# A six-layer transformer on one core: four of the repeated slots written out, and the hand order changed on every engine

## The reference

```python
xn = layernorm(x)
s = xn
for i in range(6):
    h = layernorm(s, ln1_w[i], ln1_b[i])
    q, k = softmax(h @ wq[i], over head dim), softmax(h @ wk[i], over tokens)
    s = (q @ (k.T @ (h @ wv[i]))) @ wo[i] + bo[i] + s      # 8 heads of 16
    h = layernorm(s, ln2_w[i], ln2_b[i]) @ w1[i]
    s = leaky_relu(h, 0.01) @ w2[i] + s                    # 128 -> 512 -> 128
logits = xn @ router_w.T + router_b
y = (xn @ expert_w[top1].T + expert_b[top1]) * max(softmax(logits))
out = x + s * silu(y)
```

## Time and profile before

| | |
|---|---|
| median of 3 runs | 595.34 us (593.69 to 601.31) |
| the profiled execution | 596.75 us, of which its span is 594.9 us |
| mean granted TensorE clock | 0.994 |
| PE busy | 578.7 us, 97% of the span |
| PE weight loads busy | 516.3 us, 87% |
| DVE busy | 540.1 us, 91% |
| ACT busy | 434.8 us, 73% |
| POOL busy | 311.1 us, 52% |

### The profile page before, as it was taken

One profiled execution on the slowest core, in us unless ns is written; L12 is line 12 of the kernel. 1 busy time (PEld: TensorE's weight loads), 2 busy tenths in 40 slices (PEclk: granted clock), 3 DMA queues, 4 the chain that ended last, 5 costly groups with the idle time before them and its releaser, 6 DMA issues.

```text
span 594.9 us, 12614 instructions
## 1 busy us (share of the span) xinstructions
PE 578.7 (97%) x4166; PEld 516.3 (87%) x4166; DVE 540.1 (91%) x1352; ACT 434.8 (73%) x763; POOL 311.1 (52%) x308
## 2 busy tenths in 40 slices
PE   7999999999999999999999999999999999999897
PEld 7899897887978889889889898898898898898796
DVE  6887999999988999999999999999999999988865
ACT  2658595876976868868768768768779678687652
POOL 5896134755852772442442532433523766867752
PEclk9989999999999999999999999999999999999999
DMA  8209233323224154445435435445342351441102
GB/s 282 75 10 328 72 110 121 124 94 130 95 84 152 71 152 146 112 133 169 124 123 163 109 141 150 116 163 158 103 165 80 108 167 57 129 156 62 45 36 106
DMA packets 74946, 73.20 MB, mean 123 GB/s; under 512 B 27265, under 2 KB 65153, under 8 KB 74882
## 3 DMA queue, kind: packets, MB, share of 16 engines
q1 hardware_dynamic: 72400, 68.18, 35.6%
q0 software_dynamic: 2048, 4.20, 2.3%
q10 hardware_dynamic: 434, 0.02, 0.0%
HBM read 39.87 MB, written 32.51 MB: 122 GB/s over the span
## 4 chain that ended last, share of the span: by engine, by line
PE 75%; DVE 11%; DMA 4%; issue 3%; POOL 3%; ACT 2%; SPq 1%; DVEq 0%; ACTq 0%; POOLq 0%
PE psY L513 23%; PE psH L406 6%; PE psS L558 6%; PE psH L407 6%; PE psH L408 6%; PE psT L592 6%; PE psT L401 6%; PE psT L526 5%; PE psM L538 5%; DVE st L1295 2%; PE psS L455 2%; DMA through<-blocks 1%; DVE X L1563 1%; DVE hid L1553 1%; DMA turned<-through 1%
## 5 line engine op out<-in xcount | busy, mean ns | idle before, releaser
L513 PE MATMUL psY<-w_all,hid 128*128 128x128 f32 x1536 | 188.7, 276 | 2.5 <-DVE hid L1553 1.8
L513 PEld LDWEIGHTS psY<-w_all,hid 128*128 128x128 f32 x1536 | 182.0, 193 | 6.6 <-issue 2.3
L1553 DVE TENSOR_TENSOR hid<-psH,hsl 128x512 f32<-128x512 f32 x192 | 127.2, 676 | 13.6 <-ACT hsl L936 13.1
L936 ACT ACTIVATE hsl<-psH 128x512 f32<-128x512 f32 x192 | 108.3, 591 | 42.0 <-PE psH L408 38.5
L2038 POOL TENSOR_TENSOR rstd<-veps,minus_half 128x8 f32<-128x8 f32 x44 | 72.7, 1653 | 61.2 <-DVE veps L1312 61.0
L2134 POOL TENSOR_TENSOR qsm<-qe,qrec 128x1024 f32<-128x1024 f32 x24 | 46.5, 1938 | 97.8 <-DVE qrec L1636 97.8
L2112 POOL TENSOR_TENSOR xn_lo<-xn,xn_hi 128x512 fp32r<-128x512 f32 x48 | 60.6, 1282 | 69.4 <-ACT xn_hi L1000 69.4
L406 PE MATMUL psH<-xn_hi,w_hi 128*128 128x512 f32 x192 | 86.4, 450 | 3.7 <-DVE hid L1553 3.4
L966 ACT ACTIVATE xh<-X,shift,rstd 128x128 f32<-128x128 f32 x188 | 77.0, 482 | 8.9 <-POOL shift L2041 8.7
L408 PE MATMUL psH<-xn_lo,w_hi 128*128 128x512 f32 x192 | 76.1, 396 | 0.0
L407 PE MATMUL psH<-xn_hi,w_lo 128*128 128x512 f32 x192 | 76.0, 396 | 0.0
(11 more groups left out here) (161 smaller groups left out, 1024.9 us busy)
## 6 DMA issues: line engine op xcount, KB each, us to landing
through<-turn SPq DMA_DIRECT2D x22, 512.0 KB, 2.7
turn<-through SPq DMA_DIRECT2D x88, 128.0 KB
through<-blocks SPq DMA_DIRECT2D x20, 512.0 KB, 3.2
turned<-through SPq DMA_DIRECT2D x80, 128.0 KB, 2.8
wb<-expert_rows SPq DMA_DIRECT2D x40, 128.0 KB, 2.0
sorted_x<-blocks SPq DMA_DIRECT2D x5, 512.0 KB, 4.4
xs_xsT<-sorted_x SPq DMA_DIRECT2D x40, 64.0 KB, 2.5
sorted_y<-ys SPq DMA_DIRECT2D x10, 256.0 KB, 2.4
```

What stands on the lines that cost most here:

```text
L513: last = nc.tensor.matmul(tile(psY, t), tile(hid[:, c, :], t), w2_all[:, n // NBATCH, c, :], start=(c == 0 and t == 0), stop=(c == NC - 1) ...
L936: nc.scalar.activation(hsl[:, i % 2, :], psH[:, i % 2, :], ACT.Copy, scale=SLOPE) \
L1553: nc.vector.tensor_tensor(hid[:, i % NC, :], psH[:, i % 2, :], hsl[:, i % 2, :], ALU.max) \
```

## The change

The helpers stay as they are; the calls are put in another order. On every engine the loop of slots ends at 20, and slots 20 to 23 are written out. POOL, DVE, PE, ACT and SP also have another order in the head, in the tail, and (POOL and DVE) inside the repeated slot. PE's set of calls is the same one, 618 of them. One `...` line stands for what is left out.

SP, the head:

```diff
-            sp.dma_start(w1_all[:, 0, :], w1[0]).then_inc(sig("ffn_first_loaded"), 16)
...
-            zero_rows()
             gather_expert_rows()
+            feature_major2(1)
+            zero_rows()
             sp.dma_start(w1_all[:, 1:L, :], w1[1:L].rearrange("l p f -> p l f")).then_inc(sig("ffn_loaded"), 16)
-            feature_major2(1)
-            feature_major2(2)
             for l in range(1, L):
                 sp.dma_start(w2_all[:, l, :, :], w2[l].rearrange("(p c) d -> p c d", c=NC)) \
                     .then_inc(sig("ffn_loaded"), 16)
+            feature_major2(2)
             feature_major1(4)
```

The head on PE and on DVE (pieces):

```diff
             first_items_by_feature(0)
+            normalised_tiles(0, 0)
             output_bias(0)
-            normalised_tiles(0, 0)
             keys(0)
...
-            attention(6)
             hidden(5, 0)
+            attention(6)
             hidden(5, 1)
             hidden(5, 2)
```

```diff
+            nc.vector.memset(eighths[:, :], 1.0 / H).then_inc(sig("ones_ready"), 1)
             input_statistics(0)
-            nc.vector.memset(ones256[:, :], 1.0)
             input_statistics(1)
             first_norm1_half(0)
...
+            add_y(1, 0)
+            leaky(1, 5)
             finish_mix(3)
-            leaky(1, 5)
             first_rows()
-            add_y(1, 0)
...
+            leaky(5, 0)
             add_attention(6)
-            leaky(5, 0)
-            leaky(5, 1)
             statistics2(6)
             key_maxima(7)
+            leaky(5, 1)
```

The repeated slot on POOL after (DVE's has `leaky(s - 3, 5)` ahead of `finish_mix(s - 1)` and `stage_w1` behind `add_attention`):

```diff
+                low_part(s - 3, 0)
                 if s % NBATCH == 3 and s < ITEMS:
                     split_w1(s // NBATCH)
-                low_part(s - 3, 0)
+                deviations2(s - 2)
                 low_part(s - 3, 1)
-                deviations2(s - 2)
```

PE in slot 20: `apply_expert(9)` stands behind `hidden(17, 3)` instead of ahead of `hidden(17, 0)`, and DVE's `expert_bias(9)` behind `variances1(20)`. PE in slots 20 to 22, as in slot 21 here:

```diff
             output(18, 2)
-            context(20)
             hidden(18, 4)
+            context(20)
             hidden(18, 5)
-            mixing(20)
             output(18, 3)
+            mixing(20)
             queries_by_feature(20)
```

The tail on ACT, DVE and POOL (pieces):

```diff
             slope(21, 4)
+            slope(21, 5)
             silu(0)
-            slope(21, 5)
+            silu(1)
+            queries_by_feature(23)
             slope(21, 6)
-            queries_by_feature(23)
```

```diff
             add_y(22, 1)
+            gated(2)
             leaky(23, 2)
             leaky(23, 3)
-            gated(2)
             leaky(23, 4)
             last_output(0)
```

```diff
             low_part(22, 1)
+            weigh(2)
+            deviations2(23)
             weigh(3)
-            deviations2(23)
-            add_input(0, 1)
             low_part(23, 0)
             low_part(23, 1)
             add_last_input()
+            add_input(0, 1)
             add_input(1, 2)
             add_input(2, 4)
```

More of the change, by code:

```diff
@@ L706, in _ @@
             output(2, 1)
+            output_bias(4)
+            keys_by_token(4)
             output(2, 2)
@@ L844, in slot @@
                 hidden(s - 3, 7)
-            for s in range(10, 24):
+            for s in range(10, 20):
                 slot(s)
+            attention(18)
+            output(16, 4)
+            output(16, 5)
+            output(16, 6)
+            output(16, 7)
+            hidden(17, 0)
+            hidden(17, 1)
+            keys(19)
+            hidden(17, 2)
+            hidden(17, 3)
+            apply_expert(group_of(20))
+            queries(19)
+            keys_by_token(19)
+            output(17, 0)
@@ new lines, in _ @@
+            output(17, 1)
+            key_sums(19)
+            hidden(17, 4)
+            hidden(17, 5)
+            output(17, 2)
+            context(19)
+            output(17, 3)
+            mixing(19)
+            queries_by_feature(19)
+            hidden(17, 6)
+            hidden(17, 7)
+            attention(19)
+            output(17, 4)
+            output(17, 5)
+            output(17, 6)
+            output(17, 7)
+            hidden(18, 0)
+            hidden(18, 1)
+            keys(20)
@@ new lines, in _ @@
+            output(18, 6)
+            output(18, 7)
+            hidden(19, 0)
+            hidden(19, 1)
+            keys(21)
+            queries(21)
+            hidden(19, 2)
+            hidden(19, 3)
+            keys_by_token(21)
+            output(19, 0)
+            output(19, 1)
+            key_sums(21)
+            output(19, 2)
+            output(19, 3)
+            context(21)
+            hidden(19, 4)
+            mixing(21)
+            hidden(19, 5)
+            queries_by_feature(21)
@@ new lines, in _ @@
+            hidden(19, 6)
+            hidden(19, 7)
+            attention(21)
+            output(19, 4)
+            output(19, 5)
+            output(19, 6)
+            output(19, 7)
+            hidden(20, 0)
+            hidden(20, 1)
+            keys(22)
+            queries(22)
+            output(20, 0)
+            hidden(20, 2)
+            hidden(20, 3)
+            keys_by_token(22)
+            output(20, 1)
+            output(20, 2)
+            hidden(20, 4)
+            key_sums(22)
@@ new lines, in _ @@
+            mask_context(20)
+            blocks_of_norm1(21)
+            leaky(18, 4)
+            leaky(18, 5)
+            add_y(18, 0)
+            finish_mix(20)
+            statistics1(22, 0)
+            leaky(18, 6)
+            leaky(18, 7)
+            add_attention(20)
+            statistics2(20)
+            add_y(18, 1)
+            statistics1(22, 1)
+            leaky(19, 0)
+            leaky(19, 1)
+            key_maxima(21)
+            variances1(22)
+            query_maxima(21)
```

642 lines of the change are left out of this document (434 added, 208 removed).

## The result

| | before | after |
|---|---|---|
| median | 596.27 us of 17 runs (593.69 to 601.31) | 600.97 us of 17 runs (598.58 to 602.24) |
| the profiled execution, its span | 596.75, 594.9 | 599.31, 597.5 |
| DVE busy | 540.1 | 546.7 |
| PE busy | 578.7 | 579.8 |

The ratio is 1.0072, with a 95% interval of 1.0056 to 1.0089: the change costs 4.3 us (0.72% of 596.3; the medians lie 4.7 apart), within 2% but clear of zero. The median is above the range of the forecast, whose value was 595.2.

What follows compares the result with a forecast made beforehand. PE was taken to bound the middle, leaving some 9 us of its idle time elsewhere; 0.5 - 1.3 + 0.6 + 0 - 0.8 - 0.5 + 1.4 = -0.1 gave 595.2 us from a median of 595.34, range 589.5 to 600.0.

Steps and rivals of the forecast that it cites:

- The middle, 0: Repeated slots: no change, since PE bounds them and the moved calls still come in time; upper bound +1 us.
- The start, +0.5: Start: keys(0) at 14.65 instead of 14.10, bias matmuls coming after the tiles; between 0 and 0.7, taken as +0.5 us.
- The head, -1.3: Head: waits of output(1, 4), hidden(5, 2) and others shrink, less 0.7 for item 4; -1.3 us, from -3.5 to +2.
- more changes of kind: PE: 115 broken-off runs of hidden instead of 107, at 0.08 us each; +0.6 us.
- A full DMA queue: Rival, head: moved weight loads delay item 4's DMAs and keys(4); 599.3 if ending at 90; chance 0.15, shared with other new waits.
- Slots 20 to 23, -0.8: Slots 20 to 23: fewer gathers beside feature_major1's DMAs, so less waiting for xnT; -0.8 of 1.44 us, range -1.4 to +1.
- The tail: Tail: context(23)'s wait goes, -0.49 us; the 1.76 stays, weigh(2) replacing weigh(3); gated(2), held by POOL, adds +1.4.
- The clock: Rival: PE's clock dips twice, once behind the 1.76 us stall; one fewer gives 593.3, one more 597.1; inside the forecast's 0.55.

Runs made afterwards that it cites:

- head_alone: The kernel before with only the changed kernel's head, all calls ahead of slot 10 on every engine: 595.61 us, ratio 0.9995 to before.
- late_alone: The kernel before with only the changed kernel's slots 20 to 23 and tail: 595.75 us, ratio 1.0007 to before.
- gated_back: The changed kernel with before's repeated slot and with gated(2) behind leaky(23, 3) again: 595.91 us, ratio 1.0012 to before.
- after_middle_of_before: The changed kernel with the repeated slot of before on DVE and POOL: 595.57 us, ratio 1.0006 to before.
- before_weigh_behind_norm: Before with weigh(3) behind deviations2(23) and, by a wait, DVE's half of norm2(23), and silu(3) behind hidden_input(23): 595.58 us, ratio 0.9996.

## Why the prediction was wrong

**The middle, 0: the step that failed.** It should have been +4. I looked at two of the edits in the repeated slot, deviations2 ahead of the second low_part and finish_mix behind a leaky, and asked whether the moved thing was still in time. It was. I didn't cost the third edit, stage_w1 behind add_attention, at all, and I didn't ask what would now run at the same time: with low_part(s - 3, 0) ahead of split_w1, POOL no longer waits for the cast but runs beside it. My upper bound, "each 0.1 us counts ten times, so +1", took all ten slots for alike. Three aren't. In them DVE has the cast to do too. What it can be held for without cost is some 0.4 us (0.7 where it comes in early), and before's one hold of 0.45 had used that up in slot 11. The measured growth of the three is 4.0 us. What I needed was at hand: DVE busy 241.32 of 252 us in the middle, the 1.87 us of the earlier trace rows, and, in the trace though not among my rows, a cast with POOL waiting for it in slots 11, 15 and 19. I had used the hold twice for the tail and not once for the stretch that repeats.

The Trainium skill, page "SBUF — State Buffer", section "SBUF: two separate sides", names two kinds of VectorE work that exclude GpSimd: with two SBUF inputs, and in a mode that uses two ports, which, it says, a float32 copy from SBUF to SBUF triggers. The trace agrees for a copy that also converts (float32 to fp32r): 1.69 us beside low_part, 0.62 us at the same place beside a short one. That it is held is shown; in which mode it runs the trace doesn't say. I had only thought of operations with two inputs.

**The start, +0.5.** keys(0) starts at 15.00 instead of 14.10, +0.9. xh of the first items comes at 11.39 on DVE instead of 10.49, because x of the second sequence lands later and its bn_stats, which stand ahead of it, start at 8.63 instead of 7.71. DVE in the kernel after:

```profile
8.63 1.64 DVE L1517 BATCH_NORM_STATS2 st<-xraw 128x6 f32<-128x128 f32 x8 [1.23 <-DMA xraw<-in_x_dram]
```

I had given nothing for DVE there, and thought that it would even be earlier. The first DMAs on SP and ACT are in another order too; which of them delays that tile, and how the 0.9 divides between this and the order of tiles and bias, isn't shown. By attention(0) only 0.1 of it is left.

**The head, -1.3.** Not shown, and in these two traces for the wrong stretches: attention(8) is 0.8 us earlier, but from attention(0) to attention(3) 1.5 us are lost and from there to attention(7) 2.6 won. The wait ahead of output(1, 4) and the one ahead of hidden(5, 2) are gone, and attention(6) waits 0.32 for its copy, where I had charged 0.34:

```profile
168.70 2.02 PE L601 MATMUL psT<-mix,qsmT 128*128 128x128 f32 x16 [0.32 <-ACT qsmT L1134]
```

head_alone can't be told from before. Over all traces attention(8) starts at 209.6 to 211.7 us with before's head (216.1 in one with a further piece at the lower clock) and at 210.2 to 212.4 with after's, so the 0.8 isn't a gain that can be claimed. The *more changes of kind* are there, 107 and 115 runs of hidden in the two traces, but what they cost wasn't measured by itself.

**A full DMA queue.** It didn't happen. The last of the weights' DMAs was issued by 79 us, seven ahead of the next tile's, and xnT(4) starts at 98.47, inside the 98 to 99.5 that I had given:

```profile
74.65 4.33 SPq L371 DMA_DIRECT2D w_all<-in_w_dram  x5
...
86.34 0.33 SPq L329 DMA_DIRECT2D through<-turn  x1
```

**Slots 20 to 23, -0.8.** The idle time there went from 1.44 to 0.70 us, as said, 0.57 of it still ahead of keys(22). The time didn't follow: the stretch from attention(19) to (22) got 0.6 us longer, since attention(22) now stands later among PE's calls, and at equal clock attention(19) to the last output takes 0.4 us more than before. late_alone, at 1.0007, agrees.

**The tail.** Both readings of the hold were right in place, and nearly in size. context(23) no longer waits. weigh(2) took weigh(3)'s place, and the 1.76 stayed; gated(2), 1.22 us in the earlier trace rows, was held, and hidden(23, 4) waited 1.04, where I had said 1.4:

```profile
563.55 1.87 DVE L1498 TENSOR_TENSOR sdev<-st 128x8 f32<-128x8 f32 x1
...
581.47 2.65 DVE L1717 TENSOR_TENSOR gate<-gate,X 128x1024 f32<-128x1024 f32 x1
...
563.48 1.92 POOL L2390 TENSOR_TENSOR gate<-gate,top_weight 128x1024 f32<-128x1024 f32 x1
...
580.67 8.02 POOL L2447 TENSOR_TENSOR xraw<-xraw,gate 128x1024 f32<-128x1024 f32 x3
...
566.64 0.51 PE L415 MATMUL psH<-xn_hi,w_hi 128*128 128x512 f32 x1 [1.76 <-DVE hid L1747]
...
584.87 0.47 PE L415 MATMUL psH<-xn_hi,w_hi 128*128 128x512 f32 x1 [1.04 <-DVE hid L1747]
```

But the cause named for gated(2), its place in DVE's list, wasn't enough, as gated_back showed, and a wait of 1 or 2 us there isn't worth its size: the tail's waits replace one another.

**The clock.** I had put the lower clock in the tail behind the 1.76 us stall. after, after_middle_of_before and gated_back have a stall of that length in the same place and keep 1.00; before and late_alone have it and don't. So the stall alone doesn't decide it. One piece less was worth 1.6 us in the tail, near the 1.9 that I had said, and it is what made the traces differ by 2.6 us instead of 4.3.

**The range.** Its upper end, 600.0, came from the DMA queue. The bound for the middle should have been worked out for the worst slot: two holds of about 1.3 us each, the length of a low part, less the 0.4 to spare, in three slots, are +6.6, and the upper end 601.8.

## What to carry to other kernels

When two engines' orders in a repeated slot are changed, lay both timelines over each other for each kind of slot that occurs, and add up how long one engine holds the other; a slot with additional work has less to spare than its neighbours, and its price counts on its own. If a wait keeps two engines apart, ask what removing or overtaking it lets run together. And measure what the slots can take with some operations added for nobody: a stage that looks bound by one engine may have a second one 0.3 us behind it. Compare a stretch of two traces only when the granted clock is the same in both: here a difference of 1.8 us was 1.6 of clock.

## What the hardware showed that I had not expected

A DVE operation with a single tensor input from SBUF was held too: the cast to fp32r (0.62 us, up to 1.71) and the tensor_scalar of last_norm2_half (four in 1.11 us, 4.86 beside POOL; besides the tensor it reads two scalars per partition). In the changed kernel, the six casts:

```profile
L1701 DVE CAST w_hi<-w_all x6: 621/1162/1706, 36.6 to 513.0; 128x512 fp32r<-128x512 f32 x6
```

POOL was held in turn: in before_weigh_behind_norm weigh(3) took 2.81 us instead of 1.9; it started at 566.04, during DVE's gated product of 1.22 us from 565.88. DVE's products that read one input from PSUM kept their length: the two leaky behind gated(2) in the changed kernel take 1.28 us beside the 8.02 us of POOL's adds, as the earlier trace rows has them with 0.676 each.
